# Attention: value products of two slots ahead of the maxima's spreading, and the shift evicted by ScalarE between the second group's two squares

## The reference

```python
qkv = (x @ w_qkv.T + b_qkv).reshape(b, n, 3, h, hd).transpose(2, 0, 3, 1, 4)
q, k, v = (qkv[0], qkv[1], qkv[2])
qgr, _ = jnp.linalg.qr(q)
kgr, _ = jnp.linalg.qr(k)
attn_grass = jnp.einsum('bhnd,bhmd->bhnm', qgr, kgr) ** 2 * grassman_scale
dots = jnp.einsum('bhnd,bhmd->bhnm', q, k)
attn_eucl = dots * scale
attn_riem = dots ** 2 * riem_scale
a = jnp.concatenate([attn_eucl, attn_riem, attn_grass], axis=1)
...
a = jnp.einsum('oc,bcnm->bonm', conv_w, a) + conv_b[None, :, None, None]
a = jax.nn.softmax(a, axis=-1)
out = jnp.einsum('bhnm,bhmd->bhnd', a, v)
```

## Time and profile before

| | us |
|---|---|
| median of 3 runs | 908.42 (908.27 to 909.32) |
| time of the profiled execution | 910.35 |
| its span | 908.7 |
| busy in the span: TensorE matmuls / VectorE / GpSimd / ScalarE | 798.0 / 719.1 / 506.5 / 439.6 |

### The profile page before, as it was taken

How to read it: one execution, slowest core, us unless ns; L and a number is a source line. 1 busy time by engine, 2 the same in 40 slices (tenths; PEclk the granted TensorE clock), 3 DMA queues, 4 the chain that set the end, 5 groups by cost and what they waited for, 6 DMA issues and landing times. The chain is left out here.

```text
span 908.7 us, 39105 instructions
## 1 busy us (share of the span) xinstructions
PE 798.0 (88%) x16294; PEld 564.3 (62%) x16294; DVE 719.1 (79%) x1291; ACT 439.6 (48%) x902; POOL 506.5 (56%) x551
## 2 busy tenths in 40 slices
PE   3577857899896599999999999999999998799994
PEld 2233325555544477877778777777777776366663
DVE  4488895488798589999899998999998997376772
ACT  2233332211192165655555655555655555277773
POOL 3256571111000578888888888888888885122220
PEclk9578887799998599999999999999999999599998
DMA  8767200022330122222221122222222220001111
GB/s 289 273 212 248 84 1 0 9 54 54 81 88 1 53 70 62 63 62 67 76 63 62 62 65 72 69 62 63 62 64 76 66 62 22 1 18 29 29 28 33
DMA packets 64289, 64.85 MB, mean 71 GB/s; under 512 B 36825, under 2 KB 54812, under 8 KB 64156
## 3 DMA queue, kind: packets, MB, share of 16 engines
q1 hardware_dynamic: 63628, 61.24, 21.8%
q10 hardware_dynamic: 528, 1.54, 0.5%
HBM read 52.93 MB, written 6.75 MB: 66 GB/s over the span
## 5 line engine op out<-in xcount | busy, mean ns | idle before, releaser
L1169 ACT ACTIVATE sq<-ps_dot 128x376 f32<-128x376 f32 x384 | 165.0, 482 | 148.4 <-PE ps_dot L1066 148.4
L1066 PE MATMUL ps_dot<-q_st,k_blk 64*64 64x94 f32 x6144 | 170.5, 249 | 1.0 <-ACT sq L1169 0.8
L1066 PEld LDWEIGHTS ps_dot<-q_st,k_blk 64*64 64x64 f32 x6144 | 134.6, 134 | 46.5 <-issue 28.8
L999 POOL TENSOR_TENSOR v_blk<-v_rep,vmask 128x384 f32<-128x384 f32 x128 | 106.6, 853 | 12.9 <-PE ps_m L1096 7.3
L1014 POOL TENSOR_TENSOR half<-prob 128x564 f32<-128x564 f32 x64 | 75.5, 1180 | 60.5 <-ACT prob L1164 60.5
L1021 POOL TENSOR_TENSOR k_blk<-k_cm,hmask 128x768 f32<-128x768 f32 x64 | 96.8, 1513 | 1.1 <-PE ps_a L1108 1.1
L1023 POOL TENSOR_TENSOR k_mix<-k_cm,cols 128x768 f32<-128x768 f32 x64 | 96.8, 1513 | 0.0
L1192 DVE TENSOR_REDUCE row_max<-ps_a 128x94 f32<-128x564 f32 x128 | 88.8, 736 | 3.6 <-PE ps_a L1116 3.5
L367 PE MATMUL ps_spread<-parts,pair_sel 128*128 128x376 bf16 x256 | 58.1, 369 | 34.5 <-DVE prod L477 22.8
L1116 PE MATMUL ps_a<-sq,mix_w 64*32 64x282 f32 x2048 | 82.6, 404 | 0.3 <-ACT sq L1169 0.3
L1161 ACT ACTIVATE prob<-prob,head_const 128x564 f32<-128x564 f32 x64 | 49.1, 768 | 67.0 <-DVE prob L1214 67.0
(11 more groups left out here) (228 smaller groups left out, 1525.3 us busy)
## 6 DMA issues: line engine op xcount, KB each, us to landing
v_rep<-v_rows SPq DMA_DIRECT2D x128, 192.0 KB, 3.0
x_g<-in_x_dram SPq DMA_DIRECT2D x15, 1500.0 KB, 6.6
v_rows<-tok SPq DMA_DIRECT2D x16, 192.0 KB
q_st<-q_cm SPq DMA_DIRECT2D x64, 47.0 KB, 1.8
out_dram<-rows SPq DMA_DIRECT2D x16, 188.0 KB
x_g<-in_x_dram ACTq DMA_DIRECT2D x1, 1500.0 KB, 7.7
top_rows<-tok SPq DMA_DIRECT2D x16, 32.0 KB
top<-top_rows SPq DMA_DIRECT2D x1, 512.0 KB, 3.4
```

Of the source, the lines that this page charges most:

```text
L999: vb = pool.tensor_tensor(v_blk[:, a, b].rearrange("p t (o d) -> p (t o) d", o=H), v_rep[:, a, b].rearrange("p (t o d) -> p (t o) d", o=H, ...
L1066: mm = pe.matmul(ps_dot[64 * v:64 * v + 64, (2 * g + b) % 3, N * c:N * c + N], k_blk[rows, a, SLOTS * (3 * v + g) + c].rearrange("p k h m ...
L1169: act.activation(sq[:, b, :, g, :], ps_dot[:, (2 * g + b) % 3, 0:SLOTS * N].rearrange("p (c n) -> p c n", c=SLOTS), ACT.Square).then_inc(s ...
```

## The change

TensorE: `attended` takes the slots that it shall handle. The first two of the six now stand ahead of `spread_max`, directly behind the dot products of group 1, and with them the waits of the whole function; the other four, and the denominators, stay behind it. VectorE: the instruction that makes `shift` is gone; the waits for it stay. ScalarE: the same addition, as an Identity activation with the constant as its bias, stands between the two squares of group 1. It waits for the spreading and, from the second pair on, for the subtractions of the pair before.

```diff
-            def attended(j, a):
-                pe.wait_ge(s["exp_done"], 2 * j + 2)
-                pe.wait_ge(s["v_ready"], j + 1)
-                if j:
-                    pe.wait_ge(s["out_done"], j)
-                for t in range(NT):
+            def attended(j, a, slots):
+                if 0 in slots:
+                    pe.wait_ge(s["exp_done"], 2 * j + 2)
+                    pe.wait_ge(s["v_ready"], j + 1)
+                    if j:
+                        pe.wait_ge(s["out_done"], j)
+                for t in slots:
...
                 dots(i, a, 1)
+                if i >= 2:
+                    attended(i - 2, a, range(0, 2))
                 if i >= 1:
                     spread_max(i - 1)
                 if i >= 2:
-                    attended(i - 2, a)
+                    attended(i - 2, a, range(2, NT))
                     denominators(i - 2)
...
+            def shifted(prev):
+                act.wait_ge(s["max_spread"], prev + 1)
+                if later(prev, 1):
+                    act.wait_ge(s["sub_done"], 3 * prev)
+                act.activation(shift[:], bass.AP(ps_a[:].tensor, 512 + REST, [[4 * 512, 128], [1024, 2], [1, N]]),
+                               ACT.Identity, bias=k["head_const"][:]).then_inc(s["shift_done"], 1)
+
-            def squares(i, g):
+            def squares(i, g, batches=(0, 1)):
                 act.wait_ge(s["dots_done"], 3 * i + g + 1)
-                for b in range(2):
+                for b in batches:
...
-                squares(i, 1)
+                squares(i, 1, (0,))
+                if has_prev:
+                    shifted(i - 1)
+                squares(i, 1, (1,))
...
             steps(act, step)
+            shifted(PAIRS - 1)
...
             def shifted(prev, a):
-                dve.wait_ge(s["max_spread"], prev + 1)
-                dve.tensor_scalar(shift[:], bass.AP(ps_a[:].tensor, 512 + REST, [[4 * 512, 128], [1024, 2], [1, N]]), k["head_const"][:], None, ALU.add).then_inc(s["shift_done"], 1)
                 dve.wait_ge(s["shift_done"], prev + 1)
```

More of the change, by code:

```diff
@@ L1152, in _ @@
             for j in (PAIRS - 2, PAIRS - 1):
-                attended(j, j % 2)
+                attended(j, j % 2, range(NT))
                 denominators(j)
```

## The result

The changed kernel takes 913.95 us (median of 4 runs, 912.17 to 916.02), the kernel before 908.35 beside it: a ratio of 1.0057, 95% interval 1.0033 to 1.0080. It is slower by 5.6 us, and a ratio of 1 lies outside the interval; 9.3 were forecast, within a range of 3 to 13.

A forecast was written before the change was run, and what follows sets the result against it. VectorE's own loop was taken to set the attention step; a first subtraction 0.12 us later in 60 steps (7.2 us) plus 0.07 in 30 (2.1 us) made 9.3 us more, 917.7 us, range 911.5 to 921.0.

The forecast's parts named there:

- The bound: Attention loop: VectorE's own loop sets the 7.17 us step, with TensorE in it at turning and spreading the maxima.
- Rival 2: Attention step: TensorE paces it, denominators come 0.08 us earlier, 4.8 us less in all, 903.6 us; chance 0.03.
- The granted clock: TensorE in the attention stage: 1.00 likely kept; a clock below 1.00 would show the forecast wrong.
- more of TensorE's waits at the turned maxima: TensorE in the attention step: expected sign of a right forecast, along with its wait before the spreading gone; no size given.
- Part 1: TensorE, two slots of value products ahead of the spreading: spreading starts 0.26 us later, two tiling drains of 0.10 included.
- Rival 1: TensorE's passages between tilings are free: spreading 0.06 us late, 2.7 us less in all, 905.7 us; chance 0.06.
- Part 2: Shift on ScalarE: takes 0.42 us, gains 0.14 by itself; after the later spreading, first subtraction 0.12 us later than now.
- Part 3: ScalarE's shift in even steps: its own wait instruction adds 0.07 us, bounds 0 and 0.08; 2.1 us in all.
- the sum: Attention stage: 60 steps of 0.12 us plus 30 of 0.07, together 9.3 us more.
- a change of tiling that might be free: TensorE around the moved slots: one free passage alone gives 3.3 us more, 911.7 us; chance 0.07.

The follow-up runs named there:

- four slots: Against the kernel before: four slots of the value products ahead of the spreading, the shift still on VectorE; 935.10 us, ratio 1.0278.
- part 1 alone: Against the kernel before: two slots of the value products ahead of the spreading, the shift still on VectorE; 914.31 us, ratio 1.0057.
- part 2 alone: Against the changed kernel: all six slots back behind the spreading, the shift still on ScalarE; 904.62 us, ratio 0.9954 to the kernel before.

## Why the prediction was right, and where it was off

**The bound.** VectorE's own loop sets the period, with TensorE in it at the turning and the spreading: confirmed for the kernels before and after. A later first subtraction went into the step one for one (four slots: 0.33 us behind two slots, and 0.33 in the step, 7.19 to 7.52), and an earlier one helped until TensorE's 7.04. Rival 2 (TensorE paces the step) was wrong for the changed kernel, but its chain of 7.04 us lies only 0.05 below the odd steps of the kernel before; the prediction named no such floor. The granted clock stayed at 1.00. Another sign that it named, more of TensorE's waits at the turned maxima, came in the weight loads (15.4 us in 59 waits from 330 to 760 us, 5.3 in 29 before), not in the matmuls.

**Part 1.** The spreading was forecast 0.26 us later and came 0.25 later, with both changes of tiling paid: the products begin 0.07 before the end of the dot products (569.11 and 569.18), the spreading 0.07 before theirs. TensorEngine Tiling (Array Packing) of the Trainium skill, section Key Properties, says that a change of the mode drains TensorE; the passage that no row had shown (128*64 to 94*128) agrees, at the 0.10 us read from the others. Rival 1 is out.

**Part 2.** 0.42 us on ScalarE was forecast, 418 ns measured; the hops too fit within 0.02 (0.04 forecast both ways; 562.78 to 562.82 and 563.24 to 563.27 in the odd step). One reading was off without effect: a single square lasts 0.48 us and not half of the 0.86 of two that overlap. But given part 1 the whole of part 2 is worth nothing in the odd steps: part 1 alone and the change both start the subtraction at 1.17. The prediction had it that part 1 more than spends what part 2 gains; in fact part 1 alone costs 0.10 us a step, since the shift on VectorE stood 0.20 us behind the spreading's end (576.16 to 576.36), of which all but a hop of 0.04 could be lost first, and part 2 alone brings the subtraction forward by 0.06 to 0.15.

**Part 3.** 0.07 us in even steps was forecast, 0.08 measured (1.25 against 1.17), and shown by taking away the wait that forced it.

**The step that was off is the sum.** It took for granted that behind the first subtraction VectorE's list costs what it cost before, so that what the subtraction moves by, every step moves by. It does in odd steps: 0.10 us for 0.12 forecast. In even steps the key block's late start of 0.10 us vanished with the shift, so 0.19 forecast became 0.08: 30 x 0.11 + 30 x 0.02 = 3.9 us less than the 9.3, which leaves 5.4, beside 5.5 in the stage and 5.6 in the medians. The late start could be seen in the trace of before, as a difference of 0.10 us between even and odd steps. The prediction used a mean of 7.17, from 60 steps in 430 us, and passed over it; the steps themselves give 7.14 (7.19 and 7.09, or 449.8 / 63).

**What was luck.** The direction and the chain were earned. That the time stayed within the range was in part luck: its lower end was set for a change of tiling that might be free, 0.10 us a step, and both were paid. What filled that room was the late start of 0.10 us in every second step, which the prediction didn't know of.

## What to carry to other kernels

Before work is put ahead of a step that closes a loop through several engines, count its time with the tiling changes that it brings, and take off the wait that it fills. Here two slots would have put the spreading off by 0.48 us (0.55 less 0.07), of which 0.22 (575.56 to 575.78) filled time in which it had waited for the maxima anyway; 0.25 was measured. One slot (0.38 less 0.07) put it off by 0.09, and with the shift on ScalarE it took 904.17 us for the 913.95 of two; beside no slot ahead (904.62) its gain is within the noise. Moving an instruction to an idle engine pays only as far as the next chain (here 0.10 us a step below the mean, through TensorE) and only if what it waits for isn't delayed in the same change. A wait that the same engine has already made is worth removing: where it forced a wait instruction of its own, it cost 0.08 us each time. And compare neighbouring steps start to start before taking a mean: a difference between them is a term that a change can add or remove.

## What the runs showed of the hardware that was not expected

One instruction more in each step of VectorE's list, be it the shift of 0.40 us or a memset of one column, in the middle or at the end, made the key block of every second step start 0.10 us later (0.31 or 0.32 us behind the output's start, for 0.21), with the durations of the instructions of the step unchanged. It was there in all six kernels whose step has such an instruction, the one before among them, and in none of the six without. They are fewer cases than twelve: VectorE's list is the same in the six without and in three of the six with, so five different lists were run. The delay sits at a fixed place of the list, VectorE's 673rd record, and came in each of the loop's passes that were compared (29 of 29), never in the odd steps (0 of 28). What the engine does there is not settled.
